# Another path for the slot outputs and another order of the weight loads in a fused transformer block; part of the squares of `dispatch` on VectorE, and six matmuls that nobody reads

## The reference, cut to what matters

```python
xn  = _rms_norm(x, norm_weight)                       # x is the layer-normalised h
tok = _l2_normalize(xn); sl = _l2_normalize(slots) * scale[:, None]
logits = einsum('sd,btd->bst', sl, tok)
y = einsum('btd,bst->bsd', xn, softmax(logits, -1))   # dispatch: one vector per sequence and slot
y = einsum('sio,bsi->bso', fc1_weight, y) + fc1_bias  # every slot has weights of its own
y = gelu(y)
y = einsum('sio,bsi->bso', fc2_weight, y) + fc2_bias
out = einsum('bsd,bst->btd', y, softmax(logits, -2))  # combine
```

## Time and profile before

| | us |
|---|---|
| median of 3 runs (lowest, highest) | 1055.19 (1052.20, 1057.06) |
| the profiled execution, its own time | 1051.24 |
| its span, first to last instruction | 1049.3 |
| TensorE busy / weight loads | 794.9 / 667.3 |
| VectorE, ScalarE, GpSimd busy | 567.0, 431.8, 317.9 |
| mean granted TensorE clock | 0.828 of full |
| read from HBM | 105.77 MB |

### The profile page before, as it was taken

How to read it: one execution, slowest core, us unless ns; L and a number is a source line. 1 busy time by engine, 2 the same in 40 slices (tenths; PEclk the granted TensorE clock), 3 DMA queues, 4 the chain that set the end, 5 groups by cost and what they waited for, 6 DMA issues and landing times. The chain is left out here.

```text
span 1049.3 us, 22626 instructions
## 1 busy us (share of the span) xinstructions
PE 794.9 (76%) x7528; PEld 667.3 (64%) x7529; DVE 567.0 (54%) x1402; ACT 431.8 (41%) x1054; POOL 317.9 (30%) x325
## 2 busy tenths in 40 slices
PE   3599999996979624443355998894359999999993
PEld 2378888885968302222234676673349999999993
DVE  2637777777363201111117588886965665556662
ACT  5347676765733201110110467652704444444441
POOL 1311212110032000000000267751774555555552
PEclk9659999998555856676687899996559999999997
DMA  9391000000000799889931900003512333233321
GB/s 283 107 428 51 2 0 0 0 0 1 1 2 2 181 416 370 357 350 367 320 113 32 413 12 1 0 0 99 124 51 42 50 53 53 48 51 52 49 48 19
DMA packets 37999, 119.33 MB, mean 114 GB/s; under 512 B 7538, under 2 KB 28436, under 8 KB 33588
## 3 DMA queue, kind: packets, MB, share of 16 engines
q1 hardware_dynamic: 24980, 104.30, 27.0%
q0 software_dynamic: 10848, 12.67, 7.5%
q10 hardware_dynamic: 2112, 1.57, 0.9%
HBM read 105.77 MB, written 11.14 MB: 111 GB/s over the span
## 5 line engine op out<-in xcount | busy, mean ns | idle before, releaser
L1028 PE MATMUL psum<-flat,m_yT 64*32 64x384 f32 x624 | 47.4, 667 | 102.8 <-issue 101.4
L1645 POOL DMA_INDIRECT out_h<-x_ys,idx x55 | 87.2, 1586 | 100.0 <-ACT x_ys L1670 60.6
L1769 PE MATMUL psum<-w_pairs,x_h_hi 128*128 x330 | 101.7, 370 | 1.1 <-DVE x_h_lo L1697 1.1
L1028 PEld LDWEIGHTS psum<-flat,m_yT 64*32 64x32 f32 x624 | 17.5, 142 | 128.1 <-issue 128.1
L985 DVE COPY f_hid<-psum 128x384 f32<-128x384 f32 x16 | 8.9, 558 | 146.7 <-PE psum L1028 146.7
L1771 PE MATMUL psum<-w_pairs,x_h_lo 128*128 x330 | 82.8, 251 | 0.0
L1697 DVE TENSOR_TENSOR x_h_lo<-psum,x_h_hi 128x384 fp32r<-128x384 f32 x110 | 56.3, 553 | 38.3 <-ACT x_h_hi L1666 37.0
L1221 POOL MEMSET b_ones<- 96x96 f32 x1 | 0.2, 179 | 241.3 <-POOLq L130 241.3
L1670 ACT ACTIVATE x_ys<-x_ys,cw 128x192 f32<-128x192 f32 x55 | 25.1, 456 | 103.0 <-DVE x_ys L1708 103.0
L1769 PEld LDWEIGHTS psum<-w_pairs,x_h_hi 128*128 128x128 f32 x330 | 61.9, 188 | 3.1 <-issue 3.1
L1666 ACT ACTIVATE x_h_hi<-psum 128x384 fp32r<-128x384 f32 x110 | 48.1, 489 | 37.1 <-PE psum L1758 35.3
(11 more groups left out here) (271 smaller groups left out, 2289.2 us busy)
## 6 DMA issues: line engine op xcount, KB each, us to landing
flat<-in_slot_w SPq DMA_DIRECT2D x27, 2304.0 KB, 21.0
ring_last<-in_slot_w SPq DMA_DIRECT2D x5, 2304.0 KB, 26.9
flat<-in_moe_w SPq DMA_DIRECT2D x1, 10752.0 KB, 29.4
flat<-in_x_patches SPq DMA_DIRECT2D x4, 1536.0 KB, 15.0
out_h<-flat SPq DMA_DIRECT2D x1, 2304.0 KB, 12.2
xtab<-flat SPq DMA_DIRECT2D x4, 576.0 KB, 4.0
m_y<-in_fc_b SPq DMA_DIRECT2D x1, 1536.0 KB, 19.5
m_y<-f_y2g ACTq DMA_DIRECT2D x16, 96.0 KB
```

The source lines that it names most:

```text
L1028: mm = pe.matmul(b_h[n][r][B * c:B * (c + 1), :], g.yT[rows, k, SC * gr + c, :], w1[c // 2][rows, c % 2, k, n * N2:(n + 1) * N2], start=(k ...
L1645: pool.indirect_dma_start(out=A["out"][:, :], out_offset=bass.IndirectOffsetOnAxis(ap=g.idx[:, i:i + 1], axis=0), in_=ys[:, i % 2, :], in_ ...
L1769: pe.matmul(b_y[u % 2], h_hi[:, k, :], g.w_pairs[:, :, k, bass.ds(e, 1), :].rearrange("p two a d -> p two (a d)"), start=(k == 0), stop=False)
```

## The change

Five edits, all in layer 0.

1. **Order of the units.** The units are loaded in the order in which TensorE uses them: groups 0 and 1 parts 0 and 1, group 0 parts 2 and 3, group 2 parts 0 and 1, group 1 parts 2 and 3, and so on. Ring, size of a unit and the number of places stay.
2. **Slot outputs by way of DRAM.** `put(gr)` is now one DMA of 192 KB from 128 partitions into a table `ytab` in DRAM; `fetch(gr)` is two DMAs of 96 KB from the table into four partitions each. Both are on SyncE's queue, in a row with the unit loads. `fetch(gr - 1)` is issued after `put(gr)` and waits until `put(gr - 1)` has landed. Behind the last unit come put(6), fetch(5), fetch(6), put(7), fetch(7).
3. **Bias.** fc2's bias comes as 48 KB, and GpSimd spreads it over the 32 sequences.
4. **Half of the squares.** For every second sequence VectorE takes the sum of squares with `bn_stats`, behind the line that makes u, and five small instructions turn the 16 statistics into `ss`.
5. **Six matmuls ahead of dispatch.** At the end of attention 0 TensorE's stream has six 384-column float32 matmuls whose result nothing reads.

```diff
@@ weight units
+def use_order():
+    pairs = [(0, 0)]
+    for gr in range(NGR):
+        if gr + 1 < NGR:
+            pairs.append((gr + 1, 0))
+        pairs.append((gr, 2))
+    return [(gr, part + i) for gr, part in pairs for i in range(2)]
+ORDER = use_order()
 def load_unit(sp, A, g, u):
-    gr, part = u // PER, u % PER
+    gr, part = ORDER[u]
@@ attention0, tensor, behind steps(...)
+            pe.wait_ge(s_sub, B)
+            keep_clock(pe, g, 6)
+def keep_clock(pe, g, n):
+    pe.wait_ge(g.s_ring[0], 16)
+    for _ in range(n):
+        pe.matmul(g.ps[:, 3, 0:N_CLOCK], g.ident[:, :], g.ring[0][:, 0:N_CLOCK], start=True, stop=True)
@@ dispatch, vector
+            def spread(b, i):
+                if b % 2 == 1:
+                    item(v, s_u, b)
+                    v.bn_stats(g.stats[:, b, :], u[:, b, :]).then_inc(s_bn, 1)
+            few_steps(B, [(centre, 0), (spread, 1)])
@@ dispatch, scalar
             def square(q, i):
-                for b in range(2):
-                    act.wait_ge(s_u, q * 2 + b + 1)
+                act.wait_ge(s_u, q * 2 + 1)
...
@@ slot_ffn, sync
+            def put(gr):
+                sp.wait_ge(s_y2s, gr + 1)
+                sp.dma_start(by_group[SC * gr:SC * gr + SC].rearrange("c b r d -> (c b) r d"),
+                             y2g[:, gr % 2, :, :]).then_inc(s_put[gr % 2], 16)
+            def fetch(gr):
+                sp.wait_ge(s_put[gr % 2], 16 * (gr // 2 + 1))
+                for r in range(2):
+                    s0 = SH * r + SC * gr
+                    sp.dma_start(g.y2[s0:s0 + SC, :, :], A["ytab"][s0:s0 + SC, :, :]).then_inc(s_y2, 16)
             for u in range(NU, NGR * PER):
...
-                if u == NU:
-                    sp.dma_start(g.y2[NS:2 * NS, :, :], A["fc2_b"].unsqueeze(1).broadcast_to([NS, B, D])).then_inc(s_b2, 16)
+                if part == PER - 1:
+                    put(gr)
+                    if gr >= 1:
+                        fetch(gr - 1)
+            put(NGR - 2)
+            fetch(NGR - 3)
+            fetch(NGR - 2)
+            put(NGR - 1)
+            fetch(NGR - 1)
+            sp.wait_ge(s_y2, 32 * NGR)
@@ slot_ffn, scalar
-            def put(gr):
-                act.wait_ge(s_y2s, gr + 1)
-                for r in range(2):
-                    s0 = SH * r + SC * gr
-                    act.dma_start(g.y2[s0:s0 + SC, :, :], y2g[:, gr % 2, r, :]).then_inc(s_y2[gr % 2], 16)
@@ slot_ffn, vector, y_copy
-                    v.wait_ge(s_y2[gr % 2], 32 * (gr // 2))
+                    v.wait_ge(s_put[gr % 2], 16 * (gr // 2))
```

More of the change, by code:

```diff
@@ L69 @@
 UNROLL = 4
+N_CLOCK = 384
 def item(eng, sem, b, per=1):
@@ L255, in expert_weights @@
     g.b1_rows = hi["b"][64:66, :]
+def use_order():
[6 more added lines that the diff above has]
+ORDER = use_order()
+TURN = {unit: u for u, unit in enumerate(ORDER)}
 def load_unit(sp, A, g, u):
-    gr, part = u // PER, u % PER
+    gr, part = ORDER[u]
     src = A["slot_w1"][2 * gr + part] if part < 2 else A["slot_w2"][2 * gr + part - 2]
@@ L711, in dispatch @@
         t_ms = sb("t_ms", [T, B])
+        s_bn = sem("bn")
         (s_neg, s_u, s_sq, s_xTp, s_xTs, s_raw, s_ms, s_root, s_chain, s_scales, s_lg, s_lgT, s_cmx, s_csub, s_cexp,
@@ L738, in _, with centre @@
             v.wait_ge(s_neg, 1)
[L739 to L743, removed]
+            def centre(b, i):
+                v.scalar_tensor_tensor(u[:, b, :], g.h[:, b, :], neg_mean[:, b:b + 1], g.nw[:, :],
+                                       ALU.add, ALU.mult).then_inc(s_u, 1)
+            def spread(b, i):
[3 more added lines that the diff above has]
+            few_steps(B, [(centre, 0), (spread, 1)])
+            odd = g.stats[:, :, :].rearrange("p (q two) s -> p q two s", two=2)[:, :, 1, :]
+            m_a, m_b, var = (g.lnt[:, i, 0:NP] for i in range(1, 4))
+            v.wait_ge(s_bn, NP)
+            v.tensor_tensor(m_a, odd[:, :, 1], odd[:, :, 1], ALU.mult).then_inc(s_bn, 1)
+            v.tensor_tensor(m_b, odd[:, :, 4], odd[:, :, 4], ALU.mult).then_inc(s_bn, 1)
+            v.tensor_tensor(var, odd[:, :, 2], odd[:, :, 5], ALU.add).then_inc(s_bn, 1)
+            v.wait_ge(s_bn, NP + 3)
+            v.tensor_tensor(m_a, m_a, m_b, ALU.add).then_inc(s_bn, 1)
+            v.wait_ge(s_bn, NP + 4)
+            v.scalar_tensor_tensor(ss[:, :].rearrange("p (q two) -> p q two", two=2)[:, :, 1], m_a, D / 2, var,
+                                   ALU.mult, ALU.add).then_inc(s_bn, 1)
             v.wait_ge(s_root, 1)
@@ L925, in slot_ffn @@
         y2g = sb("y2g", [128, 2, 2, D])
+        b2 = sb("b2", [2 * NS, D])
+        s_b2w = sem("b2w")
         s_b1, s_b2, s_h1, s_hid_a, s_hid_v, s_hTp, s_hb, s_gelu, s_y2p, s_y2s = (
             sem(n) for n in ("b1", "b2", "h1", "hid_a", "hid_v", "hTp", "hb", "gelu", "y2p", "y2s"))
-        s_y2 = [sem(f"y2_{i}") for i in range(2)]
+        s_y2 = sem("y2")
+        s_put = [sem(f"put_{i}") for i in range(2)]
         b_h = [[g.ps[:, 2 * n + r, 0:N2] for r in range(2)] for n in range(2)]
@@ L936, in _ @@
             sp.dma_start(b1[:, :, :, :], A["slot_b1"].rearrange("p (g k c) -> p g k c", g=NGR, k=NCK)).then_inc(s_b1, 16)
+            sp.dma_start(b2[NS:2 * NS, :], A["fc2_b"]).then_inc(s_b2, 16)
+            by_group = A["ytab"].rearrange("(r s) b d -> s b r d", r=2)
+            def put(gr):
[7 more added lines that the diff above has]
+                    sp.dma_start(g.y2[s0:s0 + SC, :, :], A["ytab"][s0:s0 + SC, :, :]).then_inc(s_y2, 16)
             for u in range(NU, NGR * PER):
-                gr, part = (u - NU) // PER, (u - NU) % PER
+                gr, part = ORDER[u - NU]
                 if part < 2:
@@ L943, in _ @@
                 load_unit(sp, A, g, u)
-                if u == NU:
-                    sp.dma_start(g.y2[NS:2 * NS, :, :], A["fc2_b"].unsqueeze(1).broadcast_to([NS, B, D])).then_inc(s_b2, 16)
-            sp.wait_ge(s_b2, 16)
+                if part == PER - 1:
[8 more added lines that the diff above has]
+            sp.wait_ge(s_y2, 32 * NGR)
+        @block.gpsimd
+        def _(pool):
+            pool.wait_ge(s_b2, 16)
+            pool.tensor_copy(g.y2[NS:2 * NS, :, :], b2[NS:2 * NS, :].unsqueeze(1).broadcast_to([NS, B, D])).then_inc(s_b2w, 1)
+            pool.wait_ge(s_b2w, 1)
         @block.scalar
@@ L973, in _ @@
                     evacuate(gr + 1)
-                put(gr)
-            for i in range(2):
-                act.wait_ge(s_y2[i], 32 * NGR // 2)
         @block.vector
@@ L1012, in _, with landed @@
         def _(pe):
-            def landed(u):
+            def landed(gr, part):
+                u = TURN[gr, part]
                 pe.wait_ge(g.s_ring[u % NU], 16 * (u // NU + 1))
+                return g.ring[u % NU]
             def first(gr):
-                landed(PER * gr)
-                landed(PER * gr + 1)
-                w1 = [g.ring[(PER * gr + i) % NU].rearrange("p (c k f) -> p c k f", c=2, k=KQ) for i in range(2)]
+                w1 = [landed(gr, i).rearrange("p (c k f) -> p c k f", c=2, k=KQ) for i in range(2)]
                 if gr >= 1:
@@ L1045, in second @@
                 for r in range(2):
-                    landed(PER * gr + 2 + r)
+                    w2 = landed(gr, 2 + r).rearrange("p (c k d) -> p c k d", c=SC, k=FC)
                     pe.wait_ge(s_gelu, 3 * gr + 2 + r)
```

10 lines of the change are left out of this document (5 added, 5 removed).

## The result

Over 20 runs of each, the median went from 1052.47 to 1051.59 us, where 1029 was forecast. The changed kernel's runs fall into two groups: six at 1036.8 to 1041.7 (median 1038.6) and fourteen at 1048.5 to 1055.4 (median 1052.6). The ratio 0.993 (95% interval 0.9906 to 0.9954) leaves out the slowest of the second group, so it flatters the change; "0.7% faster" is an average over two different outcomes, one of which is no gain at all. The profiled execution (1052.1, span 1050.3) is of the second group.

A forecast was written before the change was run, and what follows sets the result against it. It took dispatch as bound by half-speed TensorE, the slot stage by late weights, its end by small DMAs. 1051.24 - 16.7 (slot stage) - 10 (dispatch) = 1024.5, plus 3.95 for the median: 1028.5, said 1029; range 1010 to 1068.

The forecast's parts named there:

- The start of `first(2)`: Slot stage: with the new unit order it would begin at 363.6 us, not 387.8, a gain of 24 us.
- taking squares off ScalarE: Dispatch: gives nothing by itself, and counts only if TensorE's clock is full.
- a full clock takes pairs to about 1.1 us: Dispatch, first half: 16 pairs fall from 29.6 to about 18 us, 12 us less, net 10 after a late start.
- The step that failed: Slot stage: one group's fetch costs the load queue 3.0 us, between bounds of 1.8 and 7.6.
- my own sum: Slot stage: unit 31 lands at 503.0 + 4c, combine begins at 509.7 + 8c, against 550.38 before; equal at c = 5.1.
- c: Slot stage: queue cost in us of one group's fetch; taken as 3.0, or 7.4 by the skill page's port rule.
- My lower bound: Slot stage: a fetch costs at least 1.8 us, 49 KB an engine at a sixteenth of 428 GB/s.
- My sign: Slot stage: spacing of the later starts of `first`, 26.4 us for a fetch cost of 3, 31 for 7.6.
- The second step: Dispatch: six unread matmuls keep TensorE dense until dispatch begins, so its first half runs at full clock; chance 0.6.
- rival 3: Slot stage: in-between fetch cost, 4 to 5.5 us, giving 1040 to 1056 us; chance 0.10.
- rival 1: Slot stage: slow fetch, 5.5 to 7.6 us; 1075 us with cold dispatch, 1066 with warm first half, about 1057 both; chance 0.29.
- rival 2: Dispatch: the clock falls anyway, the six matmuls only cost 2 us, the fetch is quick: 1040 us; chance 0.24.

The follow-up runs named there:

- e6: The kernel before, with only half of the squares moved to VectorE and no unread matmuls: ten runs from 1051.04 to 1059.27 us, ratio 1.002.
- e1: The changed kernel with no fetch among the loads; one DMA after the last put brings all 64 slots: 1018.94 us, ratio 0.965.
- e11: The changed kernel with the filled dispatch of e7 and each put and fetch on ScalarE's queue instead of SyncE's: 1041.99 us.
- e5: The kernel before with only the dispatch edits (squares, six unread matmuls): three of twelve runs at 1037.9 to 1042.8 us, nine at 1051.1 to 1055.4.
- e13: The changed kernel with the filled dispatch of e7; in-loop fetches bring other data into four neighbouring slots: 1044.23 us.
- e14: e13 with the four slots of each fetch eight partitions apart, and eight rows apart in DRAM: 1017.68 us.
- e7: e1 with eight unread matmuls ahead of dispatch instead of six, and one behind the transposes of each of the first four pairs: 1008.35 us, ratio 0.959.
- e3: The changed kernel with ScalarE's direct puts into the SBUF table restored, instead of the way through DRAM: 1039.57 us, ratio 0.985.
- e12: e7 with its one fetch cut into four by sequence, combine starting on the first piece: 1006.36 us, ratio 0.955.
- e2: e1 without any fetch of the slot outputs; GpSimd fills their place with zeros: 996.18 us.
- e9: e7 with its one fetch at the end cut into sixteen of four neighbouring slots each: 1024.55 us.

## Why the prediction was wrong, and where it was right

**Right.** The start of `first(2)`, to 0.3 us. That taking squares off ScalarE gives nothing at half clock (e6). That the puts are cheap: e1's starts of `first` are 22.7 us apart with them, 22.4 + 1.0 forecast. That SyncE's wait at a fetch costs little in itself: in the three holes of the changed kernel the engines don't run dry (1.01 to 1.04 busy), and e11 clears that wait without a gain. That a full clock takes pairs to about 1.1 us (0.98): an execution that kept it is 12.8 us below one that lost it in e5 and 14.0 in the changed kernel, 12 forecast, and in e5 9.8 below the kernel before, net 10 forecast.

**The step that failed** is the price of a fetch: "I take 3.0: the long rows are like those of the units, and a destination that took 65 GB/s isn't capped at 26." It was 6.2 in the loop against e1, and 5.4 against my own sum, which had loads and puts 3.4 us too long (503.0 - 363.6 = 139.4, e1 136.0); behind the loop it was (25.4 - 6.7) / 4 = 4.7. Over the eight, (550.1 - 509.7) / 8 = 5.05, by my own sum the break-even (5.1), so the slot stage stood still. I let single slices of 61 and 65 GB/s outweigh the average of 26; the average of the whole transfer was the better row. The estimate from "SBUF — State Buffer", "Door 1: The DMA port swizzle", of the Trainium skill, c = 7.4, was nearer than mine, and e13 against e14 (6.4 and 3.0 us) agree with its rule as far as they go. My lower bound had the four engines right, 1.8 us; what I had wrong is how much longer each row takes into neighbours and amid the loads, 2.7 us on average instead of 0.91. With slots apart (e14) my 3.0 would have been right.

My sign for it was bad as well. I wrote that starts of `first` would lie "26.4 for c = 3, 31 for 7.6" apart; they lie 26.3 apart, which reads as c = 3. But of the five distances only the last three have a fetch in front: from `first(4)` on it is (495.5 - 411.3) / 3 = 28.1, against 23.0 in e1.

**The second step** is "They keep the array dense until dispatch begins." They end at 259.05, the first transpose comes at 260.55, and a thin stretch follows. I gave the full clock 0.6; it held in 6 of 20 executions, 3 of 12 in e5. "TensorE: Matmul & The Clock Gate", Part 4, of the Trainium skill, says that transposes don't count as matmuls do. From this I had concluded that the clock falls soon after the first half begins. That conclusion fails in e7, where 1.00 is granted through a stream of which a third are transposes; the page's sentence isn't tested by it, since two thirds are matmuls.

So the outcome was rival 3 with a cold clock in two thirds of the executions and a warm one in the rest, a mixture that no single case of mine described. A slip in rival 1 changes nothing of this: its 1075 leaves out the 2 us of the six matmuls that rival 2 counts.

## What to carry to other kernels

Price a small DMA by how many engines its rows fall on, by the partitions that it writes, and by what it does to the loads around it. Here rows of 24 KB into four neighbouring partitions held up full-rate loads on either queue; pieces of 768 bytes in e3 didn't, but landed late. Fetching all 64 slots behind the loads was cheapest (e1, e7, e12). When unread work is to hold a clock, look at windows of 1 us where it ends, and at several executions: one profile of the changed kernel showed a fall, one of e2 none, with the same program up to there. And choose a sign that a wrong price can't imitate: count how many of the distances contain the event.

## What was not expected of the hardware

A fetch of 197 KB into four and four neighbouring partitions took 6.2 to 6.4 us from loads that run at 427 GB/s, while DMA engines showed 1.01 busy: that share doesn't tell moving from waiting. Alone at the end, sixteen DMAs of 98 KB took 22.4 us from the first row to the last, 1.4 each, and the last half of them ran at the pace of slots apart (e9). The first eight rows took 2.1 to 3.2 us each, the last eight 0.91, as long as a row with slots apart. Why neighbours are dear amid loads and at first, and cheaper later, stays open.
